# Film products moved into the sparse attention, out biases on GpSimd, an MLP product in two token halves

## The reference, cut to what matters

```python
Q, K = x_text @ Wq, x_vision @ Wk                      # 4 heads of 32
topv, topi = top_k(scores / sqrt(32), 32)              # of 1601 keys
attn_mean = scatter(softmax(topv), topi).mean(heads)
c_t = attn_mean @ (x_vision @ Wv) * text_mask
x = layernorm(x_text, g_norm_in, b_norm_in)
scale_in, shift_in = split(c_t @ W_film_in + b_film_in)
x = x * (1 + mod_gate * scale_in) + mod_gate * shift_in
y = s4d(x, ...)                                        # a long convolution, by Fourier transforms of 128 points
scale_out, shift_out = split(c_t @ W_film_out + b_film_out)
y = y * (1 + mod_gate * scale_out) + mod_gate * shift_out
xt = x_text + y
h = gelu(layernorm(xt, g_ffn, b_ffn) @ W1 + b1) @ W2 + b2    # 512 -> 2048 -> 512
return layernorm(xt + h, g_norm_out, b_norm_out)
```

## Time and profile before

| | us |
|---|---|
| median of 3 runs | 2319.63 (2317.9 to 2322.04) |
| the profiled execution, its own time | 2316.71 |
| its span in the trace | 2315.0 |
| TensorE busy | 2108.2 (91%) |
| VectorE busy | 995.2 (43%) |
| ScalarE busy | 699.7 (30%) |
| GpSimd busy | 419.9 (18%) |

### The profile page before, as it was taken

One profiled execution on the slowest core, in us unless ns is written; L12 is line 12 of the kernel. 1 busy time (PEld: TensorE's weight loads), 2 busy tenths in 40 slices (PEclk: granted clock), 3 DMA queues, 4 the chain that ended last, 5 costly groups with the idle time before them and its releaser, 6 DMA issues. The chain is left out here.

```text
span 2315.0 us, 26087 instructions
## 1 busy us (share of the span) xinstructions
PE 2108.2 (91%) x9802; PEld 1226.4 (53%) x9802; DVE 995.2 (43%) x2013; ACT 699.7 (30%) x1382; POOL 419.9 (18%) x474
## 2 busy tenths in 40 slices
PE   7989999999999998899999997688598986899999
PEld 3545555555555543544444443333233444899998
DVE  6455645656556402420000016999764055412120
ACT  3434544444445411321111114555311112111111
POOL 0000000000000001179888611222100001000010
PEclk9999999999999999999999999889799998899999
DMA  6102121221212223378888757342250100766652
GB/s 218 41 20 74 44 73 51 72 82 39 78 43 69 70 94 155 116 292 307 306 311 323 294 182 246 124 150 82 67 236 19 42 9 16 304 239 232 240 213 79
DMA packets 130925, 327.12 MB, mean 141 GB/s; under 512 B 39617, under 2 KB 88801, under 8 KB 111474
## 3 DMA queue, kind: packets, MB, share of 16 engines
q1 hardware_dynamic: 98368, 293.59, 35.4%
q10 hardware_dynamic: 29730, 23.29, 3.1%
q0 software_dynamic: 2704, 8.59, 1.1%
HBM read 303.40 MB, written 20.91 MB: 140 GB/s over the span
## 5 line engine op out<-in xcount | busy, mean ns | idle before, releaser
L876 PE MATMUL a_mix<-a_xn,a_probs_T 128*128 128x384 f32 (+1 forms) x832 | 315.0, 496 | 14.7 <-issue 9.7
L805 PE MATMUL a_sc<-a_wk_centred,a_ctx_T 128*128 128x512 f32 x624 | 288.0, 598 | 2.3 <-DVE a_keys L463 2.3
L876 PEld LDWEIGHTS a_mix<-a_xn,a_probs_T 128*128 128x128 f32 (+1 forms) x832 | 146.7, 192 | 121.9 <-issue 74.9
L1946 PE MATMUL c_gate_up<-bc_w_wide,c_h_rows 128*128 128x512 f32 x480 | 210.9, 592 | 0.0
L805 PEld LDWEIGHTS a_sc<-a_wk_centred,a_ctx_T 128*128 128x128 f32 x624 | 117.9, 192 | 126.1 <-issue 105.2
L1850 DVE TENSOR_TENSOR c_hidden<-c_silu,c_gate_up 128x512 f32<-128x512 f32 x38 | 26.1, 688 | 360.0 <-PE c_gate_up L1946 348.1
L1946 PEld LDWEIGHTS c_gate_up<-bc_w_wide,c_h_rows 128*128 128x128 f32 x480 | 90.1, 190 | 108.1 <-issue 108.1
L2401 PE MATMUL f_ring<-f_picked_T,f_w 128*128 128x160 f32 x1024 | 143.5, 300 | 0.0
L2416 PE MATMUL f_ring<-f_hidden,f_w 128*128 128x160 f32 x1024 | 141.4, 300 | 0.8 <-ACT f_hidden L2291 0.8
L2416 PEld LDWEIGHTS f_ring<-f_hidden,f_w 128*128 128x128 f32 x1024 | 139.3, 190 | 1.4 <-ACT f_hidden L2291 1.2
L2401 PEld LDWEIGHTS f_ring<-f_picked_T,f_w 128*128 128x128 f32 x1024 | 139.9, 190 | 0.2
(11 more groups left out here) (539 smaller groups left out, 3217.6 us busy)
## 6 DMA issues: line engine op xcount, KB each, us to landing
bc_w_wide<-in_L_ffn_W SPq DMA_DIRECT2D x64, 1024.0 KB, 5.4
f_w<-in_L_ffn_W SPq DMA_DIRECT2D x32, 2048.0 KB, 8.8
c_w_down<-in_L_ffn_W SPq DMA_DIRECT2D x34, 1024.0 KB, 7.1
a_ctx_T<-in_ctx_T SPq DMA_DIRECT2D x48, 384.0 KB, 3.5
...
```

The source lines that it names most:

```text
L805: last = pe.matmul(key_bank(b, t), ctx_T[:, n % AHEAD, k, cols], wk_centred[:, k, :], start=(k == 0), stop=(k == KC - 1))
L876: ins = pe.matmul(mix[:, 0:DC], probs_T[0:m, t, p * P:(p + 1) * P], xn[0:m, b % 2, t, :], start=(t == 0), stop=(t == CT - 1))
L1946: last = pe.matmul(gate_up[2 * (u % 2) + part][:], h[:, k, :], w_wide[:, i % WIDE_RING, k, :], start=(k == 0), stop=(k == KD - 1))
```

## The change

1. The attention stage now also makes a part of the film work. A new class `Films` holds the film weights, the film biases as rows that are added by a matrix product with ones, the values of tiles 0 to 2 and `xin`, which lies in the room of `hT`. SP loads `Early` and `Films` near the start of the stage, ahead of `load_turned(2)`.
2. GpSimd makes the normalized and gained `xin` for all tiles ahead of its first subtraction (VectorE measures `hn` first), masks a tile of `c_T` when it is there (the last at the stage's end), and applies the inner scale and shift from a staging buffer, which is the first 512 columns of `average_rows`.
3. `FILMS_AT` says after which batch's `blend` TensorE makes which pieces: the values of tiles 0 to 2, their inner products and one outer product, ten pieces. ScalarE takes them behind the next batch's `exponentials(b, 1)`.
4. In each batch TensorE's order is now `score(b+2)`, `average(b)`, `keys(b+3)`, `turn_average(b)`, `blend(b)`, film pieces; ScalarE's is `exponentials(b, 1)`, the pieces, `put_scores(b+2)`, `put_shares(b)`, `exponentials(b+1, 0)`, `put_averages(b)`, `put_keys(b+3)`, `put_mean(b)`, `put_mix(b)`.
5. `context` and `context_T` have one buffer each; SP waits for the blend or the key chunk before.
6. The film stage keeps the value, inner products and transform of the last tile, and seven outer products. ScalarE copies the outer products out, and GpSimd adds the biases and `hn`; VectorE's `finish` has two operations in place of four. GpSimd also adds `b2` and `b_norm_out`.
7. The MLP's first product is made for tiles 0 and 1 and then for tiles 2 and 3. The transposes of tiles 2 and 3 stand behind the second and fourth block.
8. The last tile's mask row is kept in `keep_room`; those of the others use a part of `value_T`.

The diff's core; in the last two lists of TensorE's order only the new order is shown.

```diff
+    def stats_on_vector(self, dve, src):
+        for t in range(self.n):
+            dve.bn_stats(self.stats[:, t, :], src[:, t, :]).then_inc(self.own, 1)
+        dve.wait_ge(self.own, self.n)
+        for t in range(self.n):
+            dve.bn_aggr(self.mv[:, t, :], self.stats[:, t, :]).then_inc(self.measured, 1)
+        dve.wait_ge(self.rooted, 1)
+        dve.reciprocal(self.rstd[:], self.rstd[:]).then_inc(self.inverted, 1)
...
+        FILMS_AT = {2: (("value", 0), ("in scale", 0)),
+                    3: (("in shift", 0),),
+                    4: (("value", 1),),
+                    5: (("in scale", 1), ("in shift", 1), ("out scale", 0)),
+                    6: (("value", 2), ("in scale", 2), ("in shift", 2))}
+        PIECES = [what for b in sorted(FILMS_AT) for what in FILMS_AT[b]]
+        STAGED = [what for what in PIECES if what[0].startswith("in")]
+        stage = average_rows[:, 0:D]
...
-                par = b % 2
-                if b >= 2:
-
-                    sp.wait_ge(keys_full, NC * (b - 1))
                 for c, (lo, hi) in enumerate(CHUNKS):
-                    sp.dma_start(context_T[par][:, :, lo:hi], d["ctx_T"][b][:, :, lo:hi]).then_inc(context_T_in[par][c], 16)
+                    sp.wait_ge(keys_full, NC * (b - 1) + c + 1)
+                    sp.dma_start(context_T[:, :, lo:hi], d["ctx_T"][b][:, :, lo:hi]).then_inc(context_T_in[c], 16)
...
+                if b:
+                    sp.wait_ge(mix_full, b)
...
             load_context(0)
+            early.load(sp, d)
+            films.load(sp, d)
             load_turned(2)
-            load_context(1)
             load_turned(3)
-            load_turned(4)
-
-            for b in range(2, NB):
+            for b in range(1, NB):
                 load_context(b)
                 if b + 3 < NB:
                     load_turned(b + 3)
-            early.load(sp, d)
...
+            pool.wait_ge(q_full, 1)
+            pool.wait_ge(second.inverted, 1)
+            pool.wait_ge(early.v_in, early.v_count)
+            for t in range(NT):
+                own.did(pool.tensor_scalar(xin[:, t, :], g.hn[:, t, :], second.mv[:, t, 0:1], second.rstd[:, t:t + 1],
+                                           ALU.subtract, ALU.mult))
+            own.wait()
+            for n, op in (("g_norm_in", ALU.mult), ("b_norm_in", ALU.add)):
+                for t in range(NT):
+                    own.did(pool.tensor_tensor(xin[:, t, :], xin[:, t, :], early.long[n][:], op))
+                own.wait()
+            films.gate(pool, early.vecs)
+
+            def to_shares(b, r):
+                pool.wait_ge(exped, 2 * b + r + 1)
+                sc = scores[:, b % KEEP, r, :]
+                pool.tensor_tensor(sc, sc, left[:, r, :], ALU.subtract).then_inc(probs_ready, 1)
+
+            def mask_tokens(t):
+                pool.wait_ge(turned_out, 2 * t + 2)
+                tile, keep = c_T[:, :, t * P:(t + 1) * P], keep_room[:] if t == NT - 1 else films.value_T[:, t, 0, :]
+                own.did(pool.tensor_scalar(keep, early.mask8[:, t * P:(t + 1) * P], 1.0, 0.0, ALU.mult, ALU.add))
+                own.wait()
+                pool.tensor_tensor(tile, tile, keep.unsqueeze(1).to_broadcast([P, KC, P]), ALU.mult).then_inc(masked, 1)
+                pool.wait_ge(masked, t + 1)
+
+            def modulate(what):
+                kind, t = what
+                n = STAGED.index(what)
+                pool.wait_ge(film_staged, n + 1)
+                pool.tensor_tensor(xin[:, t, :], xin[:, t, :], stage,
+                                   ALU.mult if kind == "in scale" else ALU.add).then_inc(film_used, 1)
+                pool.wait_ge(film_used, n + 1)
+
             for b in range(NB):
-                for r in range(1 if b == NB - 1 else 2):
-                    pool.wait_ge(exped, 2 * b + r + 1)
-                    sc = scores[:, b % KEEP, r, :]
-                    pool.tensor_tensor(sc, sc, left[:, r, :], ALU.subtract).then_inc(probs_ready, 1)
+                to_shares(b, 0)
+                for kind, t in FILMS_AT.get(b, ()):
+                    if kind == "value":
+                        mask_tokens(t)
+                if b < NB - 1:
+                    to_shares(b, 1)
+                for what in FILMS_AT.get(b - 1, ()):
+                    if what in STAGED:
+                        modulate(what)
+            mask_tokens(NT - 1)
...
+            def take_film(what):
+                kind, t = what
+                act.wait_ge(film_full, PIECES.index(what) + 1)
+                src = film_bank(what)
+                if kind == "value":
+                    act.activation(films.value_T[:, t].rearrange("p k n -> p (k n)"), src, ACT.Copy,
+                                   scale=early.vecs["mod_gate"][:, 0:1]).then_inc(film_taken, 1)
+                elif what in STAGED:
+                    n = STAGED.index(what)
+                    if n:
+                        act.wait_ge(film_used, n)
+                    act.activation(stage, src, ACT.Copy).then_inc(film_staged, 1)
+                    act.wait_ge(film_staged, n + 1)
+                    act.sem_inc(film_taken, 1)
+                else:
+                    act.activation(films.outer[:, t, int(kind == "out shift"), :], src, ACT.Copy).then_inc(film_taken, 1)
+
+            act.wait_ge(early.v_in, early.v_count)
             for b in range(NB):
                 exponentials(b, 1)
...
-                if 1 <= b and b + 2 < NB:
-                    put_keys(b + 2)
+                if b < NB - 1:
+                    for what in FILMS_AT.get(b - 1, ()):
+                        take_film(what)
...
+                if b + 2 < NB:
+                    put_scores(b + 2)
                 if b < NB - 1:
                     put_shares(b)
+                if b < NB - 2:
+                    exponentials(b + 1, 0)
                 put_averages(b)
+                if b + 3 < NB:
+                    put_keys(b + 3)
                 put_mean(b)
+                if b == NB - 2:
+                    exponentials(b + 1, 0)
                 if b < NB - 1:
-                    exponentials(b + 1, 0)
                     put_mix(b)
-                if b + 2 < NB:
-                    put_scores(b + 2)
+                if b == NB - 2:
+                    for what in FILMS_AT[b][:-1]:
+                        take_film(what)
             put_mix(NB - 1)
...
+            def film(what):
+                kind, t = what
+                n = PIECES.index(what)
+                out = film_bank(what)
+                before = [i for i in range(n) if film_bank(PIECES[i]) is out]
+                if before:
+                    pe.wait_ge(film_taken, before[-1] + 1)
+                if kind == "value":
+                    if t == 0:
+                        pe.wait_ge(early.w_v_in, 16)
+                    pe.wait_ge(masked, t + 1)
+                    for m in range(KD):
+                        for k in range(KC):
+                            last = pe.matmul(out[:, m * P:(m + 1) * P], early.w_v[:, k, m * P:(m + 1) * P],
+                                             c_T[:, k, t * P:(t + 1) * P], start=(k == 0), stop=(k == KC - 1))
+                else:
+                    outer, shift = kind.startswith("out"), kind.endswith("shift")
+                    pe.wait_ge(films.gated, 4)
+                    pe.wait_ge(films.w_out_in if outer else films.w_in_in, 16)
+                    pe.wait_ge(film_taken, PIECES.index(("value", t)) + 1)
+                    last = films.product(pe, out, films.value_T[:, t], int(outer), int(shift))
+                last.then_inc(film_full, 1)
...
             for b in range(NB):
-                average(b)
-                blend(b)
                 if b + 2 < NB:
                     score(b + 2)
+                average(b)
                 if b + 3 < NB:
                     keys(b + 3)
+                turn_average(b)
+                blend(b)
+                for what in FILMS_AT.get(b, ()):
+                    film(what)
...
+    def load(self, sp, d):
+        sp.dma_start(self.w_in[:], d["L1_xattn_W_film_in"]).then_inc(self.w_in_in, 16)
+        sp.dma_start(self.w_out[:], d["L1_xattn_W_film_out"]).then_inc(self.w_out_in, 16)
+        sp.wait_ge(self.zeroed, 2)
+        for i, name in enumerate(("L1_xattn_b_film_in", "L1_xattn_b_film_out")):
+            for j in range(2):
+                at = 32 * (2 * i + j)
+                sp.dma_start(self.rows[at:at + 1, :], d[name].rearrange("(a n) -> a n", a=2)[j:j + 1, :]
+                             ).then_inc(self.rows_in, 16)
+
+    def clear(self, pool):
+        pool.memset(self.rows[:], 0.0).then_inc(self.zeroed, 1)
+        pool.memset(self.ones[:], 1.0).then_inc(self.zeroed, 1)
+
+    def gate(self, pool, vecs):
+        pool.wait_ge(self.rows_in, 64)
+        for i in range(2):
+            for j in range(2):
+                r = slice(32 * (2 * i + j), 32 * (2 * i + j) + 1)
```

(72 more changed lines are left out.)

333 lines of the change are left out of this document (156 added, 177 removed).

## The result

The changed kernel takes 2287.64 us, the median of 4 runs (2284.59 to 2291.42), against 2318.77 us of the kernel before in 4 runs beside it (2313.48 to 2322.04): a ratio of 0.9868 (95% interval 0.9852 to 0.9885). Timed again on another chip with other kernels it was 0.9885 (0.9865 to 0.9904). The forecast was 2290.0 us with a range from 2281 to 2304.

The account below looks back on a forecast made before the run. VectorE's picks were taken to bound the attention, TensorE nearly all of the film and MLP stage. Film stage -37.4 and attention +8.0 gave -29.4 us, from 2319.6 to 2290.2 us (likeliest 2290, range 2281 to 2304).

Parts of the forecast that it names:

- Start of the film stage: Film stage up to its first film product: 7.5 us in place of 17.7, so -10.2 us.
- Film and transforms: Film products and transforms: seven of 16 products go, bias products are added, 67.6 to 44.6 us, so -23.0.
- Between film and MLP, and the MLP's first product: Gap before the MLP: 8.3 to 3.6 us, -4.7; first product in halves: 56.8 to 57.3 us, +0.5.
- The new order and the single buffers: Attention stage: the new order alone, and transfers into one buffer each for context and its transpose, cost nothing.
- Rival 4: Slower than before: transfers into the single buffers come late and all six attention batches pay, past 2324 us; chance 0.05.
- The picks and the port: Port shared by VectorE and GpSimd: picks safe, normalizing and sums may be held up, 0.5 us a tile.
- VectorE's wait in batch 5's first pick and the clock: Attention: film pieces delay ScalarE's exponentials, +1.2 us (0 to 4); TensorE's low clock in late batches, +2.4 (0 to 6).
- The end: Attention's end: late film pieces delay the last average, +3.0 us (0 to 7); GpSimd's mask of the last tile, +1.4.
- GpSimd before the first batch: Attention's start: GpSimd's normalizing and gains take about 15 us from 1418, with time until 1448.
- Rival 1: Film work hides wholly beside the picks; attention grows only by GpSimd's 1.4 us: 2283.6 us; chance 0.13.
- Rival 2: Attention: VectorE waits in most batches from 3 on, +15 us: 2305 us; chance 0.16.
- Rival 3: Film stage gains less: GpSimd's outer sums come late or the halved MLP product is slower: 2297 us; chance 0.10.

Follow-up runs that it names:

- after_again: The changed kernel itself, timed again on another chip with other kernels: ratio 0.9885 (0.9865 to 0.9904) to the kernel before.
- biases_on_vector: The changed kernel with the additions of `b2` and `b_norm_out` back on VectorE: ratio 0.9865 to the kernel before.
- order_alone: The kernel before with only the attention's new order and single buffers for the context and its transpose, no film pieces: ratio 1.0003 to the kernel before.
- share_first: The changed kernel, GpSimd's subtraction for the last batch's first pick waiting until VectorE has written the last share: ratio 0.9873 to the kernel before.
- sums_twice: The changed kernel with each of GpSimd's seven sums on the outer products done twice: ratio 0.9875 to the kernel before.

## Why the prediction was right, point by point

The total was closer than its terms. 2290.0 us lies 2.4 us above the measured 2287.64, though the attention cost 3.2 us more than forecast and the film stage was right to 0.4 us; the other stages, which the change doesn't touch, made up the difference in these executions. That part is luck: beside after_again the gain was 27.3 us (2319.99 to 2292.66) and not 31.1.

**Start of the film stage.** Forecast -10.2, measured -10.9. The 24 value products of 128 columns took 4.38 us, between the 2.7 and 5.4 of the bounds and 0.6 under the 5.0 that I took; PEclk was 0.75 over the 6.8 us.

**Film and transforms.** Forecast -23.0, measured -21.7. By the starts of the groups in the trace the nine products that stay took 32.3 us where I had 31.5: two in a row took 7.06 us, as before, but one alone between transforms 3.63, and five of the nine now stand alone. The bias rows cost 1.05 and not 0.86 each, 0.4 together, and the transforms 11.5 us in place of 11.4. That is the 1.3 us. My 0.43 us for any instruction of 512 columns was too wide a reading: the average's 16 such instructions took 3.19 us at the full clock, 0.20 each, and a bias row's two 1.05.

**Between film and MLP, and the MLP's first product.** Forecast -4.7 and +0.5, measured -4.6 and -0.6. 256 instructions in 55.2 us (56.2 less 1.0 for the transposes) are 0.216 us each, under the line through 160 and 512 columns (0.219; the prediction has 0.220) and at half of 512 (0.215).

**Out biases on GpSimd: nothing.** Shown by biases_on_vector. I had written that I was wrong if VectorE waits for GpSimd's outer sums. It does, for all but the first tile, for instance

```profile
1738.55 0.69 DVE L3440 TENSOR_TENSOR d_rest<-cd_context_T,d_y 128x512 f32<-128x512 f32 x1 [3.25 <-POOL cd_context_T L3412]
```

and it costs nothing, since with each sum doubled the end stays. It is also nearly a tie: the sum ended at 1738.44 and TensorE's transform back, which VectorE needs too, at 1738.33. The check should have been for TensorE's wait, not VectorE's.

**The new order and the single buffers: nothing.** Shown by order_alone. Rival 4 falls with it: there TensorE waits for no transfer between the first and the last pick, and in the changed kernel for one, 5.66 us for the keys of batch 2 (I had some 6), for which VectorE doesn't wait.

**The picks and the port.** Picks held their time, and a normalizing beside GpSimd lost 0.6 to 0.7 us (1.15 and 1.22 in place of 0.55) where I had 0.5. Not foreseen was that a small multiplication in a pick would be locked out; it was slack here, as share_first shows.

**VectorE's wait in batch 5's first pick and the clock.** Forecast +1.2 and +2.4, together 3.6; the end of batch 6's picks came 4.7 us later after the first pick than before (215.4 against 210.8), which is the two waits of 3.41 and 1.33 us. I had allowed for one short wait and called several a sign of being wrong; there were two, the first not short. The mechanism, the value tile taken only behind the next exponentials with product, scores and average lined up behind it, was right. The size was off at its start: batch 2's average began 10.1 us after the picks' end, not 8.4 (10.2 in order_alone, so this is the new order's), and the low clock hit it, 6.04 us in place of 4.6:

```profile
1516.37 6.04 PE L3067 MATMUL d_mean<-d_scores,d_share 128*64 128x512 f32 x16 [1.72 <-ACT d_share L2933]
```

I had put the low clock into late batches. There the averages took 3.19 us in batches 3 and 6 and 4.70 and 4.89 in 4 and 5, and over all picks PEclk rose from 0.86 to 0.91. Late, the clock cost 2.9 us between the turn of batch 5's average and the average of batch 6; they went to the end of the attention and not to VectorE, so they lie in the next term.

**The end.** Forecast +3.0, measured +5.2: the last average ended 43.3 us after batch 6's picks (1674.64 less 1631.32), before 38.2 (1668.42 less 1630.27). Batch 6's own average started at 15.5, not at 10.6; the clock gave part back, with 3.2 us for the last average and not 4.5. Behind it the blend was 0.4 us shorter, and the last mask and the change of stage cost +1.8 (1682.80 to 1685.59 against 1676.99 to 1677.98) where I had +1.4. In all 4.7 + 5.2 - 0.4 + 1.8 = 11.3, before rounding 11.2, against the forecast's 8.0.

**GpSimd before the first batch.** Forecast 15 us from 1418, done 1433, with a limit at 1448: 13.5 and 28.5 us behind the first pick. It took 21.5 us from 1420.07, behind a wait for the transfer of `b_norm_in`, and was done 25.7 us behind the first pick of this execution (1441.6 less 1415.9), inside the limit by 2.8:

```profile
1420.07 8.28 POOL L2786 TENSOR_SCALAR hT<-hn,d_second_mv,d_second_rstd 128x512 f32<-128x512 f32 x4 [20.00 <-DMA d_r_b_norm_in<-in_L_xattn_b_norm_in]
1428.43 4.94 POOL L2791 TENSOR_TENSOR hT<-hT,d_r_g_norm_in 128x512 f32<-128x512 f32 x4
```

**The other rivals.** Rival 1, all hidden, is what another placing of the same pieces nearly reaches: +1.8 us up to the last copy, with 0.9851. The 68 free us did suffice; what was wrong was the place of the pieces behind batches 2 and 3. That the last 1.8 us are those behind batch 6 no run shows. Rival 2 came about in two batches, not in most from 3 on. Rival 3 is refuted by sums_twice and by the 0.216 us.
